# Two attention layers on one core: score banks that keep the maximum and add key differences, and softmax sums laid out over 128 partitions

## The reference

```
h      = group_norm(x)                      # 32 groups of 2 channels, per image
q,k,v  = Wq h + bq, Wk h + bk, Wv h + bv    # 64 channels
scores = q^T k / 8                          # 1024 x 1024 per image
attn   = softmax(scores, over keys)
x      = x + Wo (attn v) + bo
```

## Time and profile before

| | |
|---|---|
| time, median of 3 runs | 186.86 us (185.61 to 187.11) |
| span of the profiled execution, first to last instruction | 184.0 us |
| profiled execution's own time | not listed beside its span; the runs lie 1.6 to 3.1 us above it |
| TensorE (PE) busy | 174.6 us, 95% |
| VectorE (DVE) busy | 138.3 us, 75% |
| GpSimd (POOL) busy | 121.8 us, 66% |
| ScalarE (ACT) busy | 100.4 us, 55% |
| TensorE's granted clock | full in all 40 slices |

### The profile page before, as it was taken

One profiled execution on the slowest core, in us unless ns is written; L12 is line 12 of the kernel. 1 busy time (PEld: TensorE's weight loads), 2 busy tenths in 40 slices (PEclk: granted clock), 3 DMA queues, 4 the chain that ended last, 5 costly groups with the idle time before them and its releaser, 6 DMA issues.

```text
span 184.0 us, 3303 instructions
## 1 busy us (share of the span) xinstructions
PE 174.6 (95%) x1223; PEld 93.5 (51%) x1223; DVE 138.3 (75%) x208; ACT 100.4 (55%) x137; POOL 121.8 (66%) x81
## 2 busy tenths in 40 slices
PE   7778899999999999999999999999999999999993
PEld 4435545555525644455535645555535555456661
DVE  2799987779887687859875787769875588386763
ACT  3479367606656376436666476527656554466500
POOL 5265017996799929996699949996799939705000
PEclk9999999999999999999999999999999999999999
DMA  5544100500016000420025000500025100110111
GB/s 154 189 100 98 34 2 0 114 4 2 0 34 142 2 0 14 102 60 0 0 54 122 0 4 20 136 18 0 5 59 115 61 0 21 37 61 7 50 57 57
DMA packets 7103, 8.89 MB, mean 48 GB/s; under 512 B 1656, under 2 KB 4144, under 8 KB 7088
## 3 DMA queue, kind: packets, MB, share of 16 engines
q1 hardware_dynamic: 6080, 7.84, 16.9%
q10 hardware_dynamic: 1008, 0.86, 1.6%
HBM read 1.58 MB, written 1.05 MB: 14 GB/s over the span
## 4 chain that ended last, share of the span: by engine, by line
PE 82%; DVE 13%; DMA 1%; issue 1%; POOL 0%; ACT 0%; DVEq 0%; POOLq 0%
PE ps_attn L887 27%; PE ps_max L817 9%; DVE part_max L588 8%; PE ps_scores L855 8%; PE ps_scores L871 7%; PE ps_scores L857 7%; PE ps_scores L859 7%; PE ps_scores L796 3%; PE ps_misc L804 2%; PE ps_attn L894 2%; PE ps_misc L900 2%; DMA xs<-x_dram 1%; PE ps_misc L894 1%; DVE quarter_rden L628 1%; PE ps_misc L831 1%
## 5 line engine op out<-in xcount | busy, mean ns | idle before, releaser
L313 POOL TENSOR_TENSOR prob_sum<-prob_sum,probs 128x1024 f32<-128x1024 f32 x41 | 97.5, 2377 | 29.0 <-ACT probs L441 16.8
L588 DVE TENSOR_REDUCE part_max<-ps_max 128x2 f32<-128x1024 f32 x60 | 73.4, 1224 | 26.3 <-PE ps_max L818 25.8
L441 ACT ACTIVATE probs<-ps_scores 128x1024 f32<-128x1024 f32 x62 | 61.0, 1025 | 46.1 <-PE ps_scores L872 45.4
L887 PE MATMUL ps_attn<-probs,vals 128*64 128x512 f32 x224 | 54.5, 605 | 0.0
L887 PEld LDWEIGHTS ps_attn<-probs,vals 128*64 128x64 f32 x224 | 13.5, 136 | 27.8 <-issue 19.2
L871 PE MATMUL ps_scores<-q_row,ones_r 64*128 64x512 f32 x62 | 24.5, 396 | 0.5 <-ACT q_row L423 0.5
L872 PE MATMUL ps_scores<-q_row,ones_r 64*128 64x512 f32 x62 | 24.6, 396 | 0.0
L817 PE MATMUL ps_max<-back,front 64*128 64x512 f32 x31 | 13.9, 449 | 2.3 <-DVE part_max L588 1.4
L817 PE MATMUL ps_max<-cross,front 64*128 64x512 f32 x29 | 14.6, 505 | 0.3 <-DVE part_max L588 0.3
L818 PE MATMUL ps_max<-cross,back 64*128 64x512 f32 x29 | 14.6, 505 | 0.0
L818 PE MATMUL ps_max<-front,back 64*128 64x512 f32 x31 | 14.0, 450 | 0.0
(11 more groups left out here) (157 smaller groups left out, 365.7 us busy)
## 6 DMA issues: line engine op xcount, KB each, us to landing
cross<-front SPq DMA_DIRECT2D x16, 128.0 KB, 2.3
cross<-back SPq DMA_DIRECT2D x16, 128.0 KB, 2.3
rden<-quarter_rden SPq DMA_DIRECT2D x44, 32.0 KB, 1.8
xs<-x_dram SPq DMA_DIRECT2D x4, 256.0 KB, 4.6
out_dram<-xs SPq DMA_DIRECT2D x3, 256.0 KB, 2.0
rden<-quarter_rden ACTq DMA_DIRECT2D x12, 32.0 KB, 1.9
q_row<-max_rows SPq DMA_DIRECT2D x14, 2.0 KB
layer<-layers_dram SPq DMA_DIRECT2D x1, 194.5 KB, 2.7
```

Source lines behind the costliest of these rows:

```text
L313: pool.tensor_tensor(total[:, :], total[:, :], probs[t][:, :], ALU.add).then_inc(added, 1)
L441: act.activation(probs[t][:, :], scores_buffer(u, t)[:, :], ACT.Exp, scale=SCALE).then_inc(exp_done, 1)
L588: dve.tensor_reduce(part_max[u % 2][:, at:at + 2 * JS + 1:2 * JS], ps[:, :].rearrange("p (g n) -> p g n", g=2), AX.X, ALU.max, negate=True ...
L887: mm = pe.matmul(ps_attn[half * C:(half + 1) * C, :], v, probs[t][:, cols], start=(t == 0), stop=(t == TILES - 1))
```

## The change

- Score tiles 2 to 7 no longer start from an empty bank. The tiles of each bank follow one another in such an order that the next one differs from the last by a difference of keys: what stands in the bank is kept, maximum included, and the product with the key difference is added. Only tiles 0 and 1 have the row pair. The differences (`steps`) are made per unit: ScalarE drains the whole keys (`whole_keys`), VectorE subtracts (`key_steps`), ScalarE rounds (`high_steps`), VectorE takes the remainder (`low_steps`), and SP swaps both parts (`swap_steps`). For units 0 and 1 GpSimd does the subtractions.
- q and k lie in `query` and `keys` now, and the projection is four matmuls of 64 rows and 64 columns, from unit 2 on into `ps_max` instead of `ps_scores[0]`. So it waits for all eight reductions of the unit before, and max tile 0 waits until the projection is drained.
- The softmax sums of units 0 to 4 are copied by ScalarE (`copy_den`), laid out over 128 partitions by four DMAs (`fold_den`), turned into reciprocals on VectorE in one operation of 8 columns (`fold`), written to DRAM and read back over all partitions by two DMAs (`unfold_rden`). Units 5 to 7 keep the old way. GpSimd's list is unchanged in the loop.
- The order on TensorE, VectorE, ScalarE and SP is written anew. On ScalarE the drains of the projection stand behind exponential 7 and `stage_max`.

The diff, cut to its core:

```diff
+        def folds(unit):
+            return unit < LAST - 2
+
+        def rden_count(unit):
+            return 32 * min(unit + 1, LAST - 2) + 128 * max(unit + 3 - LAST, 0)
+
+        def den_read(unit):
+            return (den_copied, unit + 1) if folds(unit) else (quarter_done, 2 * (unit - LAST + 3))
...
+        def projected(unit):
+            return ps_scores[0] if unit < HEAD else ps_max
+
+        rden_line = nc.dram_tensor("rden_line", (P, TILES), F32, kind="Internal").ap()
...
+            def swap_steps(u):
+                own, other, both = keys[u % RING], cross[u % RING], slice(HALF, 3 * HALF)
+                sp.wait_ge(*low_count(steps_lo, head_steps_lo, u))
+                sp.dma_start(other[0:C, both].bitcast(F32), own[C:P, both].bitcast(F32)).then_inc(lo_swapped[u % RING], 16)
+                sp.dma_start(other[C:P, both].bitcast(F32), own[0:C, both].bitcast(F32)).then_inc(lo_swapped[u % RING], 16)
...
+            def fold_den(u):
+                sp.wait_ge(den_copied, u + 1)
+                for q in range(4):
+                    row = quarter_den[q * QUARTER:q * QUARTER + 1, :].rearrange("p (i e) -> p i e", e=TILES)
+                    sp.dma_start(den_cols[quarter(q), :], row).then_inc(den_folded, 16)
+
+            def unfold_rden(u):
+                sp.wait_ge(fold_done, u + 1)
+                if u:
+                    sp.wait_ge(rden_in, rden_count(u - 1))
+                sp.dma_start(rden_line, rden_cols[:, :]).then_inc(rden_stored, 16)
+                sp.wait_ge(rden_stored, 16 * (u + 1))
+                if u:
+                    sp.wait_ge(normed, u)
+                for n in range(2):
+                    line = rden_line[n * C:(n + 1) * C, :].rearrange("p e -> (p e)").unsqueeze(0).broadcast_to([C, HALF])
+                    sp.dma_start(rden[n * C:(n + 1) * C, :], line).then_inc(rden_in, 16)
...
             for w in range(UNITS):
-                if w:
+                if w and folds(w - 1):
+                    fold_den(w - 1)
+                    unfold_rden(w - 1)
+                elif w:
                     spread_rden(w - 1)
+                if w + 1 < UNITS:
+                    place_rows(w + 1)
                 if w + 2 < UNITS:
                     swap_hi(w + 2)
-                    swap_lo(w + 2)
-                if w + 1 < UNITS:
-                    place_rows(w + 1)
+                    swap_steps(w + 2)
...
+            def high_steps(u):
+                act.wait_ge(*low_count(k_steps, head_k_steps, u))
+                act.activation(keys[u % RING][:, STEP_HI], steps[:, CHAIN], ACT.Copy).then_inc(steps_hi, 1)
...
+                act.activation(steps[:, 0:HALF], projected(u)[:, LO], ACT.Identity,
+                               bias=k_bias[u // B][:, :]).then_inc(k_full, 1)
...
+            def copy_den(u):
+                act.wait_ge(den_mm, u + 1)
                 if u:
-                    act.wait_ge(normed, u)
-                for block in (2, 3):
-                    act.dma_start(rden[quarter(block), HALF // 2:HALF],
-                                  quarter_rden[quarter(3), :]).then_inc(rden_in, 16)
-
-            set_back(0)
+                    act.wait_ge(den_folded, 64 * u)
+                act.activation(quarter_den[:, :], ps_misc[:, 0:HALF // 2], ACT.Copy).then_inc(den_copied, 1)
...
                 exp(w, 4)
+                if 0 < w and folds(w - 1):
+                    copy_den(w - 1)
                 exp(w, 5)
-                if prep:
-                    high_front(w + 2)
-                    high_back(w + 2)
-                if 0 < w < LAST:
-                    spread_rden(w - 1)
-                if 0 < w < LAST:
+                exp(w, 6)
+                exp(w, 7)
+                if w < LAST:
                     stage_max(w + 1)
                 if prep:
+                    high_query(w + 2)
+                    high_keys(w + 2)
+                    whole_keys(w + 2)
                     bias_x(w + 2)
-                exp(w, 6)
-                exp(w, 7)
-                if w == 0:
-                    stage_max(1)
+                    high_steps(w + 2)
...
+            def key_steps(u):
+                dve.wait_ge(k_full, u + 1)
+                dve.tensor_tensor(steps[:, HALF:2 * HALF - P], steps[:, 0:HALF - P], steps[:, P:HALF],
+                                  ALU.subtract).then_inc(k_steps, 1)
+
+            def low_steps(u):
+                dve.wait_ge(steps_hi, u + 1)
+                dve.tensor_tensor(keys[u % RING][:, STEP_LO], steps[:, CHAIN], keys[u % RING][:, STEP_HI].bitcast(F32),
+                                  ALU.subtract).then_inc(steps_lo, 1)
...
+            def fold(u):
+                dve.wait_ge(den_folded, 64 * (u + 1))
+                if u:
+                    dve.wait_ge(rden_stored, 16 * u)
+                dve.reciprocal(rden_cols[:, :], den_cols[:, :]).then_inc(fold_done, 1)
...
-                reciprocal(w - 1, 0)
-                if not prep:
-                    part(w + 1, 6)
-                reciprocal(w - 1, 1)
-                if prep:
-                    part(w + 1, 6)
+                if not folds(w - 1):
+                    reciprocal(w - 1, 0)
+                part(w + 1, 6)
+                if not folds(w - 1):
+                    reciprocal(w - 1, 1)
                 part(w + 1, 7)
+                if folds(w - 1):
+                    fold(w - 1)
                 join(w + 1, neg_max[:, :])
                 if prep:
-                    low_front(w + 2)
-                    low_back(w + 2)
+                    low_query(w + 2)
+                    key_steps(w + 2)
                     part(w + 2, 0)
+                    low_steps(w + 2)
                     part(w + 2, 1)
...
-                pe.matmul(ps_scores[0][:, HI], p[first, 0:P], h[first, :], start=True, stop=True)
-                pe.wait_ge(back_set, u // B + 1)
-                pe.matmul(ps_scores[0][:, LO], back_w[u // B][second, :], h[second, :], start=True, stop=True).then_inc(proj_mm, 1)
+                ps, top, low = projected(u), slice(0, C), slice(C, P)
+                pe.matmul(ps[top, HI], p[top, WQ:WQ + C], h[top, :], start=True, stop=True)
+                pe.matmul(ps[low, LO], p[top, WK:WK + C], h[top, :], start=True, stop=True)
+                pe.matmul(ps[top, LO], p[low, WK:WK + C], h[low, :], start=True, stop=True)
+                pe.matmul(ps[low, HI], p[low, WQ:WQ + C], h[low, :], start=True, stop=True).then_inc(proj_mm, 1)
...
+                    if u >= HEAD:
+                        pe.wait_ge(q_lo, u + 1 - HEAD)
+                        pe.wait_ge(k_full, u + 1)
...
             def scores(u, t):
                 scores_main(u, t)
-                scores_row(u, t)
+                if t < 2:
+                    scores_row(u, t)
...
-                n, j = divmod(t, JS)
+                order, n = divmod(t, 2)
+                at = (JS - order) % JS * P
...
+                pe.matmul(left, key_top[top, hi], q[top, HI], start=t < 2, stop=False, skip_group_check=t >= 2)
...
+                pe.matmul(left, key_top[top, lo], q[top, HI], start=False, stop=t >= 2, skip_group_check=t >= 2)
+                mm = pe.matmul(right, key_low[low, lo], q[low, HI], start=False, stop=t >= 2, skip_group_check=t >= 2)
+                if t >= 2:
+                    mm.then_inc(scores_mm, 1)
...
             max_after(TILES + 7, 1, 7)
+            pe.wait_ge(max_done, 2 * TILES)
+            project(2)
             values(0, 4)
             values(0, 5)
             turn_max(1)
-            max_after(2 * TILES, 2, 0)
+            partial_max(2, 0)
             pe.wait_ge(max_staged, 2)
             project_v(2)
...
-                next_max(2)
+                max_after(TILES * (w + 1) + 2, w + 1, 2)
                 scores(w, 0)
                 scores(w, 1)
-                next_max(3)
+                max_after(TILES * (w + 1) + 3, w + 1, 3)
                 values(w - 1, 6)
                 values(w - 1, 7)
-                next_max(4)
+                max_after(TILES * (w + 1) + 4, w + 1, 4)
                 scores(w, 2)
                 scores(w, 3)
-                next_max(5)
+                max_after(TILES * (w + 1) + 5, w + 1, 5)
                 pe.wait_ge(v_copied, min(w + 2, UNITS))
                 denominators(w - 1)
                 values(w, 0)
-                if prep:
-                    scores(w, 4)
-                    next_max(6)
-                    scores(w, 5)
-                    pe.wait_ge(exp_done, TILES * w + 5)
-                    project(w + 2)
-                else:
-                    next_max(6)
-                    scores(w, 4)
-                    scores(w, 5)
-                next_max(7)
+                max_after(TILES * (w + 1) + 6, w + 1, 6)
+                scores(w, 4)
+                scores(w, 5)
                 values(w, 1)
                 values(w, 2)
                 values(w, 3)
-                pe.wait_ge(quarter_done, 2 * w)
```

(24 more changed lines are left out.)

325 lines of the change are left out of this document (130 added, 195 removed).

## The result

The changed kernel takes 222.49 us (median of 4 runs, 219.03 to 223.64) against 186.82 (185.61 to 187.11): ratio 1.180, 95% interval 1.170 to 1.190. The profiled execution is the shortest of the four, 219.03 us with a span of 217.2, where the sum gave a span of 202.5: 14.7 us are missing in the sum. The median lies another 3.5 us above the profiled execution; no trace shows that part.

The account below looks back on a forecast made before the run. TensorE, busy 174.6 of 184.0 us, bounded the kernel; new waits would outweigh its removed rows: 184.0 + 5.2 head + 11.2 units + 2.1 last unit = 202.5 us span, with 2.9 from span to median 205 us, range 195 to 213.

Parts of the forecast that it names:

- the sum: Whole kernel, score tile to score tile: 184.0 plus head 5.2, units 11.2 and last unit 2.1 gives a 202.5 us span.
- What bounds it, and the links of a unit: Middle unit: TensorE bound before; waits between engines then set the period, 22.7 us by VectorE or 23.2 by the reciprocals' way.
- the last part of the prediction: Signs to look for; among those of being right, GpSimd waits 3 to 5 us for the reciprocals in its finishing pass.
- one VectorE pass, at most 0.74: Low part of the steps, before reduction 1: at most 0.74 us, pitch about 0.66, putting max tile 2 at 9.3.
- Head: Up to unit 1's first score tile: 5.2 us later, at 45.5; unit 0's scores about 1.0 late for a swap.
- The fold: Softmax sums' reciprocals: fold landed at 1.9, reciprocals back at about 7.0 after max tile 7; that way sets period 23.2.
- An earlier R gains at most 0.5 per unit: R, when the reciprocals land for GpSimd (taken 7.0): earlier gains at most 0.5 us per unit, later costs its full delay.
- Rows that come out whole: Rival: TensorE stays full, the 11.5 us of removed row pairs come out nearly whole, 175 to about 178 us; chance 0.05.
- rows against waits: Rival: waits and removed rows cancel, a period of 20.3 with the head as before, 186 to 188 us; chance 0.03.
- The serial projection: Rival: the four projection tiles run one after another, 1.0 us more in each of six units, 211 us; chance 0.07.
- the fold's last piece: Lands 1.9 us after T, max tile 7's issue; rival: 1.5 us later, period 24.7, 213 us, chance 0.10.
- Tail and rows: Last unit: 2.1 us longer, six pairs less but bare reciprocals and waits; each removed row pair saves 0.24 us.

Follow-up runs that it names:

- e13: Changed kernel, TensorE's waits filled with unread products (head too), low parts of key differences on GpSimd, VectorE's first probability addition behind reduction 4: 208.9 us, ratio 1.121.
- e7: Kernel before plus only the fold of the softmax sums in five units, its transfers ahead of the swaps in SP's queue: 202.7 us, ratio 1.086.
- e1: Changed kernel plus unread products of ones in TensorE's waits, six before the first score tile, four behind max tile 1 of later units: 217.1 us, ratio 1.163.
- e2: Changed kernel with VectorE's low parts of the key differences moved behind the reduction of the next unit's second max tile: 219.7 us, ratio 1.177.
- e10: Changed kernel, fold kept, with e1's fillers and the low parts of the key differences moved from VectorE to GpSimd: 218.8 us (216.8 to 222.5).
- e14: e13 without the fold, so with the softmax sums' reciprocals made the old way in every unit: 205.1 us, ratio 1.101.
- e3: Changed kernel without the fold in any unit, so the kept score banks and the projection's new place alone: 213.2 us, ratio 1.127 against the kernel before.
- e5: e3 with e1's fillers, ten unread products of ones in TensorE's waits in the head and units: 212.2 us (209.4 to 213.8).

## Why the forecast was right in direction and wrong in size

The stations of the sum, each from first score tile to first score tile; the last column is the changed kernel with fillers and reordered, at full clock and without the three collisions in its middle units:

| stretch | forecast | changed kernel | e13 |
|---|---|---|---|
| up to unit 1 | 45.5 | 50.8 | 48.9 |
| unit 1 | 22.5 | 24.6 | 22.2 |
| units 2 to 5 | 92.8 | 98.8 | 94.3 |
| unit 6 | 16.6 | 17.7 | 17.2 |
| unit 7 to the end | 25.1 | 25.4 | 25.4 |
| span | 202.5 | 217.2 | 208.1 |

- **What bounds it, and the links of a unit: right.** Transpose, projection, drains, max tiles 0 and 1, and the landing of the reciprocals stand within about 0.1 us of the forecast in the unit shown, and so does max tile 5 in three of e13's four middle units (17.2 in the other). GpSimd waited 3.0 us, as the last part of the prediction asked for.
- **The step that failed is the price of VectorE's and GpSimd's passes, "one VectorE pass, at most 0.74".** It was read from the earlier trace rows, where the second operand is in PSUM. The new pass reads two SBUF tiles and took 1.44 to 1.59 us in five units of six; max tile 2 was late by 0.5 to 1.1 us, and TensorE's wait ahead of it was 2.0 to 2.1 where about 1.5 was forecast. Nothing in the earlier trace rows shows two such passes at once; the page of the Trainium skill cited above does state the rule, and by it this was foreseeable.
- **No term for the clock.** Before, all slices are at full clock; the sum took each row's duration into a kernel with waits of 2 us. Around waits of 2.0 to 2.5 us the granted clock fell to 0.50, for 6.8 us in the head, 6.8 at the first two and 3.4 at each of four more unit boundaries, and TensorE ran pairs at 0.42 to 0.43 us. From max tile 2 to max tile 5 the middle units took 7.8 to 9.0 us, not 7.3. Not every wait does this: one of 1.9 us in the last unit passed without it, and e7, with waits of 1.4, kept 1.000. Clock and collisions together are worth 9.1 us of span in the profiled executions (217.2 to e13's 208.1), 13.6 in the medians, though the cure of one alone gave 3 to 5 us (e1) or 1 to 3 (e2), and both together gave 4 (e10). A third meeting, first addition against GpSimd's addition and root, took the time over: it is absent in the changed kernel, whose first addition comes too late for it, and stands in four units each of e1, e2 and e10.
- **Head: mis-sized.** The first score tile, which waits for the swap of 256 KB, came 3.1 us later than before, not 1.0. Of the head's 5.3 us 2.1 lie there, 2.1 from it to max tile 7 (16.2 us where the forecast has 14.1; the clock was at half for 6.8 of them), and 1.1 behind max tile 7. In e13 3.4 us of the head stay: 2.9 ahead of the first score tile, 0.1 and 0.5. They are most of the 5.6 us by which e13's span still exceeds the sum. How much of them is the swap's size and how much ScalarE's order ahead of it was not tried apart.
- **The fold: the landing right, its worth not.** "An earlier R gains at most 0.5 per unit" compares with 0.8 to 1.0 in e13 against e14, and some 2 us a unit between the changed kernel and e3, where what collides depends on when GpSimd comes free.
- **Rivals.** Rows that come out whole, and rows against waits, needed periods under 20.4; the least measured in a middle unit with the projection in ps_max is 22.3 (e14). The serial projection did not happen, and the fold's last piece landed at T + 1.66 (forecast 1.9); in one unit it came 0.4 us late.
- **Tail and rows: right.** 25.4 against 25.1, and score pairs at full clock 0.23 us.

## What to carry to other kernels

A duration read from a row holds for its operands and for what the neighbour engine does: ask of each new VectorE pass with two SBUF inputs what GpSimd runs at that time, and which of the two begins first. A forecast that adds waits to a TensorE at 95% needs a term for the clock. And when two cures give back little each, look in their traces for what took the time over, and try them together before dropping either.

## What was not expected of the hardware

- VectorE's subtraction of two SBUF tiles of 512 columns: 0.67 us when it began 0.01 to 0.03 us ahead of a GpSimd addition (e5), 2.89 when it began 0.01 us behind one (e5), 1.44 to 1.59 beside two short GpSimd passes (changed kernel). GpSimd's root of one column: 0.55 us, or 1.53 behind the start of VectorE's addition of two SBUF tiles (e10).
- Products of ones that nobody reads raised the mean granted clock (0.921 in the changed kernel, 0.976 in e1, which differs by them alone), but when the clock has already fallen they take nearly twice their time. Eight of them, in e10, ahead of units 1 and 2:

```profile
46.79 3.67 PE L827 MATMUL ps_scores<-ones 128*64 128x256 f32 x8
72.24 1.94 PE L827 MATMUL ps_scores<-ones 128*64 128x256 f32 x8
```

- The fillers cost something at full clock too: max tile 2 stands at T + 9.6 in e10's units, with eight products, and at 9.2 in e13's, with six.
